# A four-block graph network on one core: mean layers in one fixed order, degree work inside the first block

## The reference

```python
x = LN(x + relu(x@W_self[type] + b_self[type] + segment_sum((x@W_rel[etype])[src] + b_rel, dst)))   # block 1
# block 2, three mean layers on the same edges, y starts as x:
h = mean_over_edges(y) @ W_l.T + y @ W_r.T + b
y = relu(LN(h) * g + beta) + y
x = LN(x + y)
# block 3, four GINE layers:
m = relu(y[src] + ew*We + be); agg = segment_sum(m, dst)
h = ((1+eps)*y + agg) @ W1 + b1; y = relu(relu(BN(h)) @ W2 + b2)
x = LN(x + y)
# block 4, one mean layer: h = mean(x)@W_l + b + x@W_r ; x = LN(x + h*sigmoid(h))
```

## Time and profile before

| | us |
|---|---|
| median of three runs | 1022.16 (1020.14 to 1029.8) |
| profiled execution | 1020.54, span 1018.8 |
| PE busy | 849.1 (83%) |
| DVE, ACT, POOL busy | 702.8, 516.1, 332.0 |
| share of the chain of waits | PE 70%, DVE 17%, ACT 7% |

### The profile page before, as it was taken

One profiled execution on the slowest core, in us unless ns is written; L12 is line 12 of the kernel. 1 busy time (PEld: TensorE's weight loads), 2 busy tenths in 40 slices (PEclk: granted clock), 3 DMA queues, 4 the chain that ended last, 5 costly groups with the idle time before them and its releaser, 6 DMA issues.

```text
span 1018.8 us, 13452 instructions
## 1 busy us (share of the span) xinstructions
PE 849.1 (83%) x3591; PEld 617.1 (61%) x3591; DVE 702.8 (69%) x1257; ACT 516.1 (51%) x990; POOL 332.0 (33%) x286
## 2 busy tenths in 40 slices
PE   2979788788888597891699999999999999999692
PEld 2666255556766485670466766658656766668572
DVE  7997656669645564448688768986698768875405
ACT  2376104436354332324677557765677557753622
POOL 3000645665013022133635026520754046512100
PEclk9989659779778799796799999999999999999797
DMA  5412457576125031242668128860778138741001
GB/s 113 135 30 92 117 165 231 162 228 187 35 73 189 0 97 68 64 147 66 140 162 199 51 73 228 181 186 4 213 187 202 63 112 206 182 117 42 1 1 51
DMA packets 59303, 122.24 MB, mean 120 GB/s; under 512 B 9104, under 2 KB 22706, under 8 KB 59237
## 3 DMA queue, kind: packets, MB, share of 16 engines
q0 software_dynamic: 20048, 52.18, 21.9%
q1 hardware_dynamic: 36165, 63.88, 20.7%
q10 hardware_dynamic: 3024, 5.31, 1.4%
HBM read 105.61 MB, written 15.74 MB: 119 GB/s over the span
## 4 chain that ended last, share of the span: by engine, by line
PE 70%; DVE 17%; ACT 7%; issue 4%; DMA 1%; another core or an unknown queue 0%; SPq 0%; DVEq 0%; ACTq 0%
PE ps L1009 15%; PE ps L692 13%; PE ps L986 10%; PE ps L1025 6%; PE ps L1041 6%; PE ps L845 5%; PE ps L816 4%; PE ps L942 2%; PE ps L797 2%; PE ps L684 2%; DVE st L1604 2%; DVE z_parts L1760 2%; ACT slot_recs L1103 2%; PE ps L786 1%; PE ps L861 1%
## 5 line engine op out<-in xcount | busy, mean ns | idle before, releaser
L1009 PE MATMUL ps<-z_parts,onehot_dst 128*125 128x512 f32 x664 | 204.5, 413 | 5.7 <-issue 2.0
L692 PE MATMUL ps<-w,xT 128*125 128x512 f32 x660 | 173.8, 422 | 8.2 <-DVE w L1358 4.9
L1760 DVE SCALAR_TENSOR_TENSOR z_parts<-ps,z_parts 128x512 fp32r<-128x512 f32 x216 | 147.8, 688 | 39.9 <-ACT z_parts L1257 32.0
L986 PE MATMUL ps<-x_parts,gather_lhs 128*128 x432 | 140.1, 409 | 40.6 <-DVE x_parts L1739 31.5
L1257 ACT ACTIVATE z_parts<-ps 128x512 fp32r<-128x512 f32 x216 | 128.3, 597 | 76.0 <-PE ps L986 59.5
L692 PEld LDWEIGHTS ps<-w,xT 128*125 128x125 f32 x660 | 130.3, 201 | 42.0 <-issue 10.4
L1009 PEld LDWEIGHTS ps<-z_parts,onehot_dst 128*125 128x125 f32 x664 | 110.1, 185 | 72.0 <-issue 53.7
L643 POOL DMA_INDIRECT gathered<-rel_rows,rowi x83 | 89.4, 1078 | 151.6 <-DMA rel_rows<-x_cur 96.5
L658 POOL DMA_INDIRECT queued<-node_rows,srci x60 | 95.7, 1594 | 88.2 <-ACT queued L1180 72.7
L986 PEld LDWEIGHTS ps<-x_parts,gather_lhs 128*128 128x128 f32 x432 | 78.8, 189 | 73.4 <-issue 57.4
L621 POOL TENSOR_TENSOR w<-w_stage,w 128x512 fp32r<-128x512 f32 x36 | 48.1, 1368 | 199.5 <-ACT w L1058 199.5
(11 more groups left out here) (275 smaller groups left out, 1245.2 us busy)
## 6 DMA issues: line engine op xcount, KB each, us to landing
w_stage<-in_weights SPq DMA_DIRECT2D x88, 256.0 KB
onehot_dst<-onehot_rows SPq DMA_DIRECT2D x80, 250.0 KB
onehot_rows<-onehot_dst ACTq DMA_DIRECT2D x20, 250.0 KB
gather_lhs<-edge_src_rows SPq DMA_DIRECT2D x8, 432.0 KB, 8.0
node_rows<-work SPq DMA_DIRECT2D x20, 160.0 KB, 2.0
queued<-node_rows,srci POOLq DMA_INDIRECT x116
node_rows<-work SPq DMA_DIRECT2D x20, 90.0 KB, 2.0
rel_rows<-rel_rows_out SPq DMA_DIRECT2D x10, 160.0 KB, 1.9
```

The costliest lines, as they stand in the source:

```text
L692: mm = pe.matmul(ps[0:R, bank, :], lt[:, a, k, n * R:(n + 1) * R], w[:, b, k, :], start=first and k == 0 and (a, b) == THREE[0], stop=last ...
L986: mm = pe.matmul(ps[:, 5 + t % 3, :], L[:, t, :], XS[:, a, bass.ds(s, 1), :], start=a == HI, stop=a == LO)
L1009: mm = pe.matmul(ps[0:R, d, :], S[:, j // SK % SR, j % SK, :], Z[:, g % ZR, a, :], start=False, stop=False, skip_group_check=True)
L1760: v.scalar_tensor_tensor(out=Z[:, g % ZR, LO, :], in0=of, scalar=0.0, in1=Z[:, g % ZR, HI, :].bitcast(F32), op0=ALU.max, op1=ALU.subtract) ...
```

## The change

- Block 1: the self products stand at every fourth tile; w5 and w6 come earlier, w7 inside the block. The adjacency's two parts, the block maximum, the degree rows, degrees, words and low blocks are made inside the block. The degree sums become 20 matmuls with 34 rows (`deg_rows`), one per adjacency tile, part and half; rows 0 and 32 of `deg_rows` and `bias_parts` hold the parts. GR is 23. ACT stores no one-hots in the block: each mean layer remakes and stores six groups, and SP stores the last three.
- Mean layers: tiles 0 and 1 are transposed before y0; tiles 2, 3, 4 behind y0, y1, y2. Tiles 0 and 1 of the next layer stand behind mean tiles 3 and 4.
- DVE does the whole affine part from PSUM: (h - mean) * g, then * rstd + beta, then relu plus the old row.
- The low parts of w7 to w13 are made by DVE, those of w20 and w21 stay on POOL. w13 is cast inside the first GINE layer. POOL's sum of block_in waits for the y products of mean layer 2.
- Last mean layer: w21's high casts stand behind all y casts on ACT.
- The sum, second norm and x_parts of the last mean layer are interleaved tile by tile.

Below is the diff, cut to its core. The moved functions (block_max, block_row, low_blocks, degrees, block_words) are as before but for banks and rows.

```diff
-GR = 20
+GR = 23
...
-FIRST = (1, 2, 4, 6, 8)
-SECOND = (3, 5, 7, 9, 10)
+FIRST = (1, 3, 5, 7, 9)
+SECOND = (2, 4, 6, 8, 10)
...
-MADE = (0, 5, 9, 15, NG)
-W4_AT, W5_AT, W6_AT = 4, 31, 57
-FILL_AT = [0] + [j * (TE - 4) // (NREL * NT - 1) for j in range(1, NREL * NT)]
+KEPT = NG - SR
+MADE = [KEPT * i // NL1 for i in range(NL1 + 1)]
+MAX_AT, HIGH_AT, DEG_AT = 6, (8, 13, 18, 23, 28), 62
+W4_AT, W5_AT, W6_AT, W7_AT = 4, 22, 44, 62
+FILL_AT = [4 * j for j in range(NREL * NT)]
...
-                    gp.wait_ge(c_used, min(2 * (i - 1) // 5, NCF + NCL - 1))
+                    gp.wait_ge(c_used, min(i // 3, NCF + NCL - 1))
...
-            for j in range(7, 12):
-                w_lows(j)
+            gp.wait_ge(y_out, Y_L1[2] + NT)
             for n in range(NT):
                 gp.wait_ge(x_made, XM_L1[2] + n + 1)
                 gp.wait_ge(b_made, n + 1)
                 gp.tensor_tensor(B[0:R, n, :], X[0:R, n, :], B[0:R, n, :], ALU.add).then_inc(sum_made, 1)
-            w_lows(12)
-            w_lows(13)
...
+            def deg_rows():
+                pe.wait_ge(at_made, NT)
+                pe.wait_ge(self_out, NREL * NT)
+                for h, bank in ((0, 7), (1, 5)):
+                    for s in range(NT):
+                        for a in (HI, LO):
+                            mm = pe.matmul(ps[0:DP, bank, 0:314 - 2 * h], one34[0:R, :],
+                                           AT[0:R, a, s, 313 * h:314 + 311 * h],
+                                           start=s == 0 and a == HI, stop=s == NT - 1 and a == LO)
+                mm.then_inc(deg_done, 1)
...
+                if i == DEG_AT:
+                    deg_rows()
+                    block_max()
+                if i == DEG_AT + 5:
+                    deg_columns()
+                    block_row()
+                if i == DEG_AT + 14:
+                    low_blocks()
...
-            pe.wait_ge(self_out, NREL * NT)
-            for n in range(NT):
-                for s in range(NT):
-                    mm = pe.matmul(ps[0:R, 7, n:n + 1], TC[0:R, s, n * R:(n + 1) * R], onef[0:R, 0:1],
-                                   start=s == 0, stop=s == NT - 1)
...
             def mean_layer(l, follow):
                 y_tile(l, 0)
+                x_tile(l, 2)
+                y_tile(l, 1)
                 x_tile(l, 3)
-                y_tile(l, 1)
+                y_tile(l, 2)
                 x_tile(l, 4)
-                y_tile(l, 2)
                 y_tile(l, 3)
                 y_tile(l, 4)
                 for n in range(NT):
                     z_tile(l, n)
-                    if l == 0 and n < NT - 1:
-                        (lambda: None, deg_rows, block_max, block_row)[n]()
-                    if l == 0 and n == NT - 2:
-                        low_blocks()
                 z_bias(l)
                 mean_low(l)
                 for n in range(NT):
+                    if follow and n == NT - 1:
+                        x_tile(l + 1, 0)
                     mean_tile(l, n)
-                    if follow and n >= 2:
-                        x_tile(l + 1, n - 2)
-
-            for n in range(3):
+                if follow:
+                    x_tile(l + 1, 1)
+
+            for n in range(2):
                 x_tile(0, n)
             for l in range(NL1):
...
-                if t % SK == SK - 1 and t // SK < MADE[1]:
-                    s_store(t // SK)
+                if t in HIGH_AT:
+                    if t == HIGH_AT[0]:
+                        act.wait_ge(c_out2, 3)
+                    s = HIGH_AT.index(t)
+                    nc.scalar.copy(AT[:, HI, s, :], TC[:, s, :]).then_inc(at_hi, 1)
+                if t == DEG_AT + 7:
+                    act.wait_ge(dg_made, 1)
+                    nc.scalar.copy(DGR[:, :], DG[:, :]).then_inc(dgr_hi, 1)
...
+            def normed_rows(l, roots, ready, xs):
+                root(0, roots + 1)
+                for n in range(NT):
+                    normal(X[0:R, n, :], H[0:R, n, :], n, ready + n + 1, x_made)
+                    by_degree(n, xs + n + 1)
+                    if n < NT - 1:
+                        root(n + 1, roots + n + 2)
+                    tr_high(n, XT, n, TR_MEAN[l] + n + 1)
+                    if n >= 2:
+                        y_high(5 + (n - 2) % 3, n - 2, Y_L1[l] + n - 1)
+                for n in (3, 4):
+                    y_high(5 + n % 3, n, Y_L1[l] + n + 1)
...
             w_highs(20)
             act.wait_ge(w2_done, NT * NL2)
-            for n in range(NT):
-                root(n, NT * (NL1 + 2) + n + 1)
-                normal(X[0:R, n, :], H[0:R, n, :], n, NT * (NL1 + 2) + n + 1, x_made)
-                by_degree(n, XM_L3 + n + 1)
-                if n >= 2:
-                    tr_high(n - 2, XT, n - 2, TR_L3 + n - 1)
+            normed_rows(NL1, NT * (NL1 + 2), 2 * NT, XM_L3)
             w_highs(21)
-            mean_parts(NL1)
...
+                if t in range(W7_AT + 4, W7_AT + 12, 2):
+                    w_low(7, (t - W7_AT - 4) // 2)
+                if t == MAX_AT:
+                    v.wait_ge(c_out, 4)
+                    link(v.tensor_reduce(bm[0:R, :], TCK[0:R, :, :], AX_X, ALU.max))
+                    v.sem_inc(low_made, 1)
+                if t - 3 in HIGH_AT:
+                    s = HIGH_AT.index(t - 3)
+                    v.wait_ge(at_hi, s + 1)
+                    v.tensor_tensor(AT[:, LO, s, :], TC[:, s, :], AT[:, HI, s, :].bitcast(F32),
+                                    ALU.subtract).then_inc(at_made, 1)
+                if t == DEG_AT + 5:
+                    v.wait_ge(deg_done, 1)
+                    v.tensor_scalar(DG[:, 0:313], ps[0:DP, 7, 0:313], 1.0, None, ALU.max)
+                    v.tensor_scalar(DG[:, 313:N], ps[0:DP, 5, 0:312], 1.0, None, ALU.max).then_inc(dg_made, 1)
+                    v.wait_ge(low_done, 1)
+                    v.tensor_reduce(bmx[:, :], ps[0:NB, 6, 0:R], AX_X, ALU.max).then_inc(low_made, 1)
+                if t == DEG_AT + 9:
+                    v.wait_ge(dgr_hi, 1)
+                    v.tensor_tensor(DGR[32:DP, :], DG[32:DP, :], DGR[32:DP, :].bitcast(F32), ALU.subtract)\
+                        .then_inc(dgr_made, 1)
+                if t == DEG_AT + 11:
+                    degrees()
+                    block_words()
             for i in range(NREL * NT):
                 if FILL_AT[i] + MR + 1 >= TE:
...
-            def affine_mult(l, n):
-                v.wait_ge(h_made, NT * l + n + 1)
-                link(v.tensor_tensor(H[0:R, n, :], H[0:R, n, :], ROW[0:R, 0, :], ALU.mult))
...
+            def head(l, n):
+                v.wait_ge(o_done, NT * l + n + 1)
+                stats(ps[0:R, n, :], n)
+                v.wait_ge(ln_var, v_stats(l, n))
+                v.scalar_tensor_tensor(out=H[0:R, n, :], in0=ps[0:R, n, :], scalar=mv[0:R, n, 0:1], in1=ROW[0:R, 0, :],
+                                       op0=ALU.subtract, op1=ALU.mult)
+
+            def v_stats(l, n):
+                return NT * (l + 1) + n + 1 if l < NL1 - 1 else NT * NL1 + FIRST[n]
+
+            def affine(l, n):
+                v.wait_ge(ln_sd, v_stats(l, n))
+                link(v.reciprocal(rstd[0:R, n:n + 1], sd[0:R, n:n + 1]))
+                link(v.scalar_tensor_tensor(out=H[0:R, n, :], in0=H[0:R, n, :], scalar=rstd[0:R, n:n + 1],
+                                            in1=ROW[0:R, 1, :], op0=ALU.mult, op1=ALU.add))
+
+            def finish(l, n):
+                affine(l, n)
+                v.scalar_tensor_tensor(out=X[0:R, n, :], in0=H[0:R, n, :], scalar=0.0, in1=X[0:R, n, :],
+                                       op0=ALU.max, op1=ALU.add).then_inc(x_made, 1)
+
+            def between(l):
+                w_lows(8 + 2 * l)
+                if l:
                     v.wait_ge(l_raw, 16 * LCH)
-                    for c in range(LCH // 2):
+                    for c in range(LCH // 2 * (l - 1), LCH // 2 * l):
                         set_lhs(c)
                 onehots_again(l)
+                if l < NL1 - 1:
+                    w_lows(9 + 2 * l)
+                v.wait_ge(row_in, 32 * (l + 1))
...
+                head(l, 0)
+                finish(l, 0)
+                head(l, 1)
+                finish(l, 1)
+                head(l, 2)
+                low(l + 1, 0)
+                finish(l, 2)
+                low(l + 1, 1)
+                head(l, 3)
+                finish(l, 3)
+                low(l + 1, 2)
+                y(l + 1, 0)
+                head(l, 4)
+                low(l + 1, 3)
+                finish(l, 4)
+                y(l + 1, 1)
+                low(l + 1, 4)
+                for n in range(2, NT):
+                    y(l + 1, n)
...
+            for n in range(NT):
+                head(l, n)
+                if n:
+                    scale(NT + n - 1, NT * NL1 + SECOND[n - 1])
+                affine(l, n)
+                v.wait_ge(sum_made, n + 1)
```

(8 more changed lines are left out.)

424 lines of the change are left out of this document (186 added, 238 removed).

## The result

| | before | changed |
|---|---|---|
| median, us | 1023.08 (4 runs, 1020.14 to 1029.8) | 994.12 (4 runs, 989.46 to 996.39) |
| profiled execution, span | 1020.54, 1018.8 | 996.39, 994.4 |
| granted clock, mean | 0.898 | 0.908 |

What follows compares the result with a forecast made beforehand. The prediction took PE, plus what PE waits for, to bound the kernel. Its terms summed to -40.9 us against 1020.54, giving 979.6, so 981 for the median; range 958 to 1002, own range from the terms' bounds 971 to 991.

Steps and rivals of the forecast that it cites:

- its own sign: First block: the prediction called itself wrong if the block ended before 262 or after 285 us; it expected 272.3.
- Part 1: First block (scatter): its end moves from 263.7 to 272.3 us, +8.7, with bounds of -16 and +15.
- lie beside PE's work: First block, to tile 60: added adjacency parts and block maximum are covered by PE's work; uncovered, up to 7 us.
- the four holds as they are, 24.5: First block: four stalls between ACT's casts and PE, about 6.1 us each, stay unchanged at 24.5 us.
- rival 3: First block: denser self products each cause a hold, ten more at 6.1 us, +61, time 1042; chance 0.04.
- Rival 1: First block: the holds vanish with the stores and denser triples, 24.5 us less, time 957; chance 0.12.
- Parts 2 and 3: Block end to mean layer 0, -19.2 us; then the two periods between mean layers, -14.3 and -13.1 us.
- rival 2: Mean layers: DVE becomes the bound, period 53 us, +12.6, and +3 before GINE, time 996; chance 0.20.
- Part 4: Last mean matmuls to GINE: 43.2 us falls to 35.3, -7.9.
- the row that was kept in place of the rule: Last mean to GINE: a DVE operation beside POOL's add takes 1.64 instead of 0.69 us, 0.95 more for four tiles.
- Part 5: GINE layers: weight 13 cast inside the first leaves their length the same, 0, +-1 us.
- Part 6: Last mean layer: PE waits 7 us before z, which ends at 991.5 instead of 986.55, +4.9.

Runs made afterwards that it cites:

- the run without holds: Changed kernel with the low parts of weights 8 to 12 back on POOL: 971.42 us, ratio 0.9714.
- the unedited block of set two: Block 1 of the changed kernel with weight 21 cast behind the second row tile of the last stage: 978.31 us, ratio 0.9559.
- the old ring's of set one: Block 1 of the changed kernel with 20 gather buffers instead of 23: 990.6 us, ratio 0.9668.
- the third chip: Chip where the changed kernel with low parts of weights 8 to 12 on POOL took 971.42 us; the kernel before took 998.97 there.
- the two edits of the kernel before: Kernel before with POOL waiting for a landed gather before every eighth, 1034.13 us, or a short POOL fill before every sixth, 1008.7 us.

## Why the prediction was right in sum and wrong in its first term

That the time lies in the range is in part luck: term 1 missed by 25.5 us, and the misses of the other terms, -13.2 and +4.2, took some of it back. By its own sign ("if the block ends before 262 or after 285"; it ended at 297.9) the account of the block was wrong.

**Part 1 failed: +34.2 instead of +8.7, outside its bounds.** (Its items of 2.74, 0.9, 0.66 and 2.6 also add to 6.9, not 7.4; that is nothing beside the miss.) Two steps of it did. The first is that the parts and the maximum added to DVE "lie beside PE's work" and cost nothing there; POOL was looked at only for its buffers, as "already some 20 gathers ahead". That lead was there in the kernel before, but it rested on issues of 0.95 us. The term's own value without any hold is 272.3 - 24.5 = 247.8; the run without holds ended the block at 270.5, 22.7 us later, and the seven long issues cost 24.0. This is the missing term, as far as blocks on two chips can be set against each other. It came from what the change packs onto DVE beside PE's work, whose cover was looked at for PE and not for POOL. The second step, "the four holds as they are, 24.5", was near in size and wrong in shape: one hold took their place, worth 27.4 us (297.9 - 270.5) here, 18.9 and 21.9 by the same reckoning in the unedited block of set two and the old ring's of set one. Ten more holds (rival 3) did not come, and on the third chip the same dense self products ran without one, so they do not make a hold by themselves. Rival 1 did in a way come true on the third chip: there the holds are absent from the changed kernel's block, and, if they are absent from the kernel before too, that would explain why the ratio there (0.9714) is the same; no trace shows it.

**Parts 2 and 3 were right**, within 1.0, 1.5 and 3.0 us. The first y starts 11.0 us behind the b_self matmuls (forecast 10.5, before 22.75). In a period one wait of 1.39 us is left of 3.4 forecast. Of rival 2 (DVE becomes the bound) the second period had all the work, and more than was reckoned: four of its weight parts took 5.79 us instead of 2.8, beside POOL's sums of block_in, which took 8.39 for five instead of 6.3. DVE's next statistics still waited 1.78 us for PE. DVE and POOL in the changed kernel:

```profile
418.00 5.79 DVE L1370 TENSOR_TENSOR w<-w_stage,w 128x512 fp32r<-128x512 f32 x4
418.17 8.39 POOL L644 TENSOR_TENSOR block_in<-x_cur,block_in 125x512 f32<-125x512 f32 x5 [153.11 <-DVE x_parts L1674]
```

Taking eight weight parts a period off DVE did not change the periods either. The Trainium skill's sentence (page "Perfetto Trace Analysis", section "Optimizing Scalar/DVE Operations") that moving work between these two engines might not help was right here only in that it made no difference.

**Part 4 was under-sized by 4.1 us**, and the row that was kept in place of the rule is why. DVE and POOL between the last mean matmuls and GINE, changed kernel:

```profile
446.70 0.69 DVE L1800 SCALAR_TENSOR_TENSOR work<-work,block_in 125x512 f32<-125x512 f32 x1
446.73 1.78 POOL L664 TENSOR_TENSOR work<-x_cur,be_rows 125x512 f32<-125x512 f32 x1 [2.57 <-ACT x_cur L1064]
```

In the kernel before POOL started first (468.22 against 468.86) and DVE took 1.64; now DVE starts 0.03 to 0.10 us ahead and takes 0.69 each time, and POOL takes 1.74 to 1.78, where its fifth, with no such operation of DVE beside it, takes 1.27. By the Trainium skill (page "SBUF — State Buffer", section "SBUF: two separate sides") the first to start holds the shared port; the traces agree in who pays, and its -11.7 for the part stands beside -12.0 measured. The prediction kept its row because both sides were longer in it. DVE's timeline in the kernel before has the reason:

```profile
468.14 0.68 DVE L1733 TENSOR_TENSOR work<-work,ln_rows 125x512 f32<-125x512 f32 x1
```

This operation, with two inputs in SBUF too, started 0.08 us ahead of POOL's, which then took 1.73; the next one, L1734, started behind POOL's and took 1.64. Each time it is the later one that is longer. It ends 0.14 us sooner than if it had begun when the first ended (469.95 against 468.82 + 1.27, and 470.50 against 469.95 + 0.69).

**Part 5, +4.2 instead of 0, stays open.** The first layer, with w13's casts in it, took 116.8 us against 112.4, and its clock was 0.95 against 0.97; the others 114.5, 113.1 and 110.1. In the other runs of changed kernels the first three layers take 112.6 to 116.7 us with no order in it, and in the two edits of the kernel before 111.9 to 116.2, so the 4.2 can't be put to w13.

**Part 6: +1.3 instead of +4.9.** The wait was as forecast (6.30 us for POOL; 7 forecast), but y4 ended 5.9 us nearer to GINE's end than before (forecast 4.5), and the z tiles came without a tile at half speed: five in 15.67 us, where 16.6 were reckoned.
